# Attention steps in the order piece, score, score, piece, and the sum over experts as one strided reduction

## The chip, the cores and the metric

The kernel runs on one core of one Trainium2 chip. What is measured is the device time of one execution in microseconds. Three runs of the kernel before gave 3410.56, 3414.06 and 3416.23 us; the median is 3414.06.

## What is computed

A network of two layers over 3327 nodes with 256 features. Each layer adds a graph part (a product with the adjacency, in the second layer an attention over a graph) and a feed-forward part. The change lies in the feed-forward part of the second layer alone, which begins with a causal attention of four heads and four experts:

```python
def _L1_ffn_ref(x, hl_w, hl_b, wq, wk, wv, gate_w, gate_b, ln_g, ln_b, ...):
    b, s, h = x.shape                       # nh = 4 heads of d = 64, ne = 4 experts
    sx = jnp.einsum('bsh,ndh->bnsd', x, hl_w) + hl_b[None, :, None, :]
    q = jnp.einsum('bnsd,neod->bneso', sx, wq)
    k = jnp.einsum('bnsd,nod->bnso', sx, wk)
    v = jnp.einsum('bnsd,nod->bnso', sx, wv)
    scores = jnp.einsum('bnesd,bntd->bnest', q, k) * d ** 0.5 + causal
    att = jax.nn.softmax(scores, axis=-1)
    qkv = jnp.einsum('bnest,bntd->bnesd', att, v)
    out = jnp.transpose(qkv, (0, 1, 3, 2, 4)).reshape(b, nh, s, ne * d)
    gs = jax.nn.softmax(jnp.einsum('bnsf,nef->bnse', out, gate_w) + ..., axis=-1)
    mixed = jnp.einsum('bnsed,bnse->bnsd', out.reshape(b, nh, s, ne, d), gs)
    hn = layernorm(mixed + resid, ln_g, ln_b)
    ...
```

The last lines matter here: the outputs of the four experts are multiplied by their gate and summed into `mixed`.

## The kernel before

The whole network is one program of stages that follow each other with a barrier between. `stage_attention` (line 1587) takes about two thirds of the time. It handles two heads at a time, as two lanes of 64 partitions ("head pair" hp = 0, 1). The 3328 rows of queries are cut into seven blocks: block 0 has 256 rows, blocks 1 to 6 have 512. A **unit** is one block with one expert (block 0 puts two experts in a unit), so there are 26 units per head pair and 52 in all: unit 2 is block 1 with expert 0, unit 6 begins block 2, unit 10 block 3, 14 block 4, 18 block 5, 22 block 6; the second head pair repeats this from unit 26.

Inside a unit the keys are taken in groups of 128, from the first key to the diagonal. Two groups make a **step**: block b has 2b+1 steps (block 5 has 11). In the last two steps' worth of groups, on the diagonal, the columns shrink from 512 to 384, 256 and 128.

A step consists of these parts, which every engine handles in an order written out by hand:

- a **score** (`scores(g)`, lines 1748 to 1757): four pairs of matmuls that put the scores of one group, less the row's maximum, into a slot of `psR`. ScalarE turns it into exponentials in `at_pt` (`exps`, line 1840), of which there are four buffers. The scores of a step are those of the next step's groups.
- **values** (`values(g)`, line 1769): exponentials times V, into `psO`. Two groups a step, at its end.
- a **piece** (`row_max`, line 1730): the row's maximum must be known before its scores are made. So a step also computes, for the unit after next, cheap scores of one 128-row tile against 512 keys, into a slot of `psR`; VectorE takes the maximum over each lane (`at_mx`, line 1899). Most steps have two pieces, a few have three. `max_pieces(u, k, half)` gives the first piece for half 0 and the rest for half 1.
- **turns**: keys "k", queries "q", row of maxima "r", and output "t". They go through `psX`. The row of maxima and the two output turns fall in steps 1 and 2 of a unit, the query in its last step. For a query or key ScalarE makes the high half and VectorE the low half (lines 1888 and 1883).
- at the end of a unit VectorE takes the output out of `psO` (`take_out`, line 1920) and then the maxima over pieces (`maxima`, line 1909).
- GpSimd adds each group's exponentials to `at_acc` (lines 2026 and 2029), two additions a step; in the last two units VectorE does it.
- the **gate**, once per block, in the first unit of the next block: part 0 (step 2 of a long unit; VectorE, lines 1947 to 1960), part 1 (step 3; ScalarE, VectorE, and GpSimd's multiplication of the experts' outputs by their weights, line 2036), part 2 (step 4; VectorE sums the experts, adds the sum to `hn`, and takes statistics, lines 1971 to 1982). VectorE does a part behind the two maxima of its step. In blocks of three steps the parts fall elsewhere: block 0's parts 1 and 2 in step 0 of unit 3.

`psR` has three slots, which scores and pieces use in turn: `slot_users()` lists the users in order of issue, and `take_slot` makes the matmuls of each user wait until the user three places before it has been read (a score by its exp, a piece by its maximum):

```python
            i = slot_of[user]
            if i >= SLOTS:
                what, before = users[i - SLOTS]
                pe.wait_ge(p1_read if what == "max" else e_ready, before + 1)
```

## Time and profile before

| | before |
|---|---|
| median of three runs | 3414.06 us (3410.56 to 3416.23) |
| the profiled execution | 3411.35 us, its span 3409.6 us |
| mean granted TensorE clock in it | 0.938 |
| TensorE busy | 3022.5 us, 89% |
| VectorE busy | 1882.0 us, 55% |
| GpSimd busy | 1783.4 us, 52% |
| ScalarE busy | 1284.8 us, 38% |
| GpSimd's additions into `at_acc` | 674, mean 2159 ns |
| VectorE's maxima of pieces | 784, mean 1112 ns |
| exps | 776, mean 944 ns |

The table is a mean over all stages. Matmuls are pipelined, so a busy TensorE may still issue late; how far two matmuls start apart tells more than how long each is shown.

### The profile page before, as it was taken

To read this page: it belongs to the slowest core of one execution; us is meant where nothing else is said; L and a number is where in the kernel's file an instruction comes from. 1 tells how busy PE (TensorE), PEld (TensorE's weight loads), DVE (VectorE), ACT (ScalarE), POOL (GpSimd) and SP (SyncE) were. 2 spreads that over 40 slices of the span, in tenths; PEclk is the share of its full clock that TensorE was granted. 3 is DMA by queue.
4 is the path that set the end of the run, shared out by engine and by line. 5 is a ranking of instruction groups with operands and counts; after the bars stand their busy time and mean duration, and the time that the engine had idled before them with its cause. 6 is when DMAs were issued, how large, how long until landed. Compare 5 with 4: busy or idle time off the path is not lost. (4 is left out here: it accounts for less than half of the span.)

```text
span 3409.6 us, 46365 instructions
## 1 busy us (share of the span) xinstructions
PE 3022.5 (89%) x18170; PEld 1857.4 (54%) x18170; DVE 1882.0 (55%) x2869; ACT 1284.8 (38%) x1712; POOL 1783.4 (52%) x957
## 2 busy tenths in 40 slices
PE   7998987589998899999999999789899999999953
PEld 3467656378875555555545555455555554545532
DVE  3545764477833456564565641255656465565566
ACT  2232320355533234334434344233343443434433
POOL 0030020332311366777888889546777878888014
PEclk9999888899998899999999999889999999999976
DMA  9961100399960000000000000000000000000001
GB/s 390 423 233 48 55 1 8 112 295 268 267 118 3 1 1 1 1 1 1 1 1 1 1 1 1 1 1 1 1 1 1 1 1 1 1 1 1 1 3 40
DMA packets 63607, 195.24 MB, mean 57 GB/s; under 512 B 8228, under 2 KB 24994, under 8 KB 53411
## 3 DMA queue, kind: packets, MB, share of 16 engines
q1 hardware_dynamic: 38642, 147.98, 11.3%
q0 software_dynamic: 24752, 44.31, 7.2%
q8 instruction: 149, 2.44, 0.3%
q14 instruction: 64, 0.52, 0.0%
HBM read 188.86 MB, written 3.41 MB: 56 GB/s over the span
## 5 line engine op out<-in xcount | busy, mean ns | idle before, releaser
L2029 POOL TENSOR_TENSOR at_acc<-at_acc,at_pt 128x1024 f32<-128x1024 f32 (+3 forms) x674 | 1455.1, 2159 | 271.5 <-ACT at_pt L1840 197.1
L1899 DVE TENSOR_REDUCE at_mx<-at_psR 128x2 f32<-128x1024 f32 (+3 forms) x784 | 859.8, 1112 | 812.4 <-PE at_psR L1730 527.7
L1840 ACT ACTIVATE at_pt<-at_psR 128x1024 f32<-128x1024 f32 (+3 forms) x776 | 728.5, 944 | 971.9 <-PE at_psR L1751 624.3
L1769 PE MATMUL at_psO<-at_pt,v 128*64 128x512 f32 (+3 forms) x3104 | 697.8, 571 | 9.8 <-DVE at_oT L1920 9.8
L1748 PE MATMUL at_psR<-at_qhi,at_klo 64*128 64x512 f32 (+2 forms) x1552 | 344.3, 439 | 68.2 <-DVE at_mx L1899 61.9
L1730 PE MATMUL at_psR<-at_khi,at_qhi 64*128 64x512 f32 (+3 forms) x1568 | 341.8, 430 | 38.8 <-DVE at_mx L1899 9.0
L1769 PEld LDWEIGHTS at_psO<-at_pt,v 128*64 128x64 f32 x3104 | 190.7, 137 | 326.6 <-issue 271.1
L1316 PE MATMUL ga_acc<-h,ga_ring 128*128 128x257 f32 (+1 forms) x1352 | 305.1, 386 | 30.1 <-ACT ga_ring L1210 26.6
L1748 PEld LDWEIGHTS at_psR<-at_qhi,at_klo 64*128 64x128 f32 x1552 | 149.8, 188 | 323.5 <-issue 304.4
L1316 PEld LDWEIGHTS ga_acc<-h,ga_ring 128*128 128x128 f32 (+1 forms) x1352 | 257.9, 193 | 75.6 <-ACT ga_ring L1210 34.7
L1748 PE MATMUL at_psR<-at_qlo,at_khi 64*128 64x512 f32 (+2 forms) x1552 | 298.8, 380 | 0.0
L1751 PE MATMUL at_psR<-at_nm,at_ones_r 64*128 64x512 f32 (+2 forms) x1552 | 297.8, 378 | 0.0
L1748 PE MATMUL at_psR<-at_qhi,at_khi 64*128 64x512 f32 (+2 forms) x1552 | 297.8, 378 | 0.0
L1730 PEld LDWEIGHTS at_psR<-at_khi,at_qhi 64*128 64x128 f32 x1568 | 162.3, 189 | 169.9 <-issue 147.6
L1189 POOL DMA_DIRECT2D ga_ring<-in_adjT x91 | 110.2, 1381 | 250.9 <-DVE ga_ring L1252 245.7
L345 PE MATMUL gc_acc<-gc_cols,gc_xs 128*128 128x512 f32 x416 | 184.0, 605 | 21.7 <-DVE gc_xs L413 13.1
L1751 PEld LDWEIGHTS at_psR<-at_nm,at_ones_r 64*128 64x128 f32 x1552 | 151.0, 189 | 27.6
L1748 PEld LDWEIGHTS at_psR<-at_qhi,at_khi 64*128 64x128 f32 x1552 | 151.0, 190 | 27.1
L1210 ACT ACTIVATE ga_ring<-ga_ring,f 128x512 f32<-128x512 f32 (+1 forms) x182 | 114.7, 682 | 128.7 <-DMA ga_ring<-in_adjT 128.7
L1748 PEld LDWEIGHTS at_psR<-at_qlo,at_khi 64*128 64x128 f32 x1552 | 151.7, 191 | 12.9
L2026 POOL COPY at_acc<-at_pt 128x1024 f32<-128x1024 f32 x50 | 52.8, 1055 | 183.8 <-PE at_psX L1715 103.1
L345 PEld LDWEIGHTS gc_acc<-gc_cols,gc_xs 128*128 128x128 f32 x416 | 80.8, 195 | 124.1 <-issue 114.6
(331 smaller groups left out, 3442.3 us busy)
## 6 DMA issues: line engine op xcount, KB each, us to landing
gc_rows<-in_adj SPq DMA_DIRECT2D x26, 1664.0 KB, 17.4
ga_rows<-in_adj SPq DMA_DIRECT2D x26, 1664.0 KB, 10.0
ga_ring<-in_adjT POOLq DMA_DIRECT2D x78, 512.0 KB, 23.7
gc_cols<-in_adjT SPq DMA_DIRECT2D x26, 1024.0 KB, 14.9
gc_ring<-in_adjT SPq DMA_DIRECT2D x26, 512.0 KB, 8.0
gc_ring<-in_adjT SPq DMA_DIRECT2D x13, 256.0 KB, 2.8
ga_ring<-in_adjT POOLq DMA_DIRECT2D x13, 256.0 KB, 9.3
out_x<-X SPq DMA_DIRECT2D x6, 512.0 KB
```

The costliest lines, as they stand in the source:

```text
L345: ins = pe.matmul(acc[:, b, c, :], xs[:, t, c * P:(c + 1) * P], cols[:, t % COLS, b * BLK:(b + 1) * BLK], start=(t == 0), stop=(t == NT - 1))
L1189: pool.dma_start(ring[:, k, :, 0:w], srcT[:, k, :, c0:c0 + w], accum_op=ALU.add).then_inc(pair_added[k], 16)
L1210: ins = act.activation(ring[:, k, j, 0:w], ring[:, k, j, 0:w], ACT.Exp, bias=f20[:, 2 * k + j:2 * k + j + 1])
L1316: ins = pe.matmul(acc[:, bank(b, s), 0:DM + 1], ring[0:r, k, j, s * P:(s + 1) * P], h1[0:r, 2 * k + j, :], start=(k + j == 0), stop=last)
L1730: ins = pe.matmul(psR[:, slot, l, 0:w], qhi[lanes[l], u % 3, s * P:(s + 1) * P], khi[lanes[l], kc:kc + w], start=True, stop=not diag)
L1748: pe.matmul(packed(psR[:, slot, l, 0:w], g), left[lanes[l], kc:kc + P], columns(right[lanes[l], u % 3, :], g), start=first, stop=False)
L1751: ins = pe.matmul(packed(psR[:, slot, l, 0:w], g), ones_r[lanes[l], :], columns(nm[lanes[l], u % 2, :], g), start=False, stop=not diag)
L1769: ins = pe.matmul(columns(psO[lanes[l], :], g), v1[:, t, (2 * hp + l) * D:(2 * hp + l + 1) * D], packed(pt[:, g % PTS, l, 0:w], g), start= ...
L1840: act.activation(pt[:, g % PTS, :, 0:w], psR[:, slot_of["score", g] % SLOTS, :, 0:w], ACT.Exp).then_inc(e_ready, 1)
L1899: dve.tensor_reduce(mx[:, u % 2, :, s, c:c + 1].rearrange("p l o -> p (l o)"), psR[:, slot_of["max", i] % SLOTS, :, 0:w], AX.X, ALU.max).t ...
L2026: pool.tensor_copy(to, got).then_inc(added, 1)
L2029: pool.tensor_tensor(to, to, got, ALU.add).then_inc(added, 1)
```

## The change

The part of a step that issues scores and pieces goes from score, first piece, score, other pieces to first piece, score, score, other pieces. `slot_users()` follows, so the slots are handed out in the new order, and each user waits for another one. VectorE's and ScalarE's own orders of maxima and exps stay. In the gate's part 2, the two additions over experts become one `tensor_reduce` over a view whose innermost axis is the expert, written to a new tile `at_mixed`; the last block of the second head pair keeps two additions, of which the second writes `at_mixed`.

```diff
@@ slot_users
-            for half in range(2):
-                if g + 2 + half < FIRST[NU]:
-                    out.append(("score", g + 2 + half))
-                out += [("max", piece[0]) for piece in max_pieces(u, k, half)]
+            out += [("max", piece[0]) for piece in max_pieces(u, k, 0)]
+            out += [("score", x) for x in (g + 2, g + 3) if x < FIRST[NU]]
+            out += [("max", piece[0]) for piece in max_pieces(u, k, 1)]
@@ stage_attention, tiles
+        mixed = m.sb("at_mixed", [P, SUB, P])
@@ TensorE
-                        for half in range(2):
-                            if g + 2 < ng:
-                                scores(g + 2 + half)
-                            for piece in max_pieces(u, k, half):
-                                row_max(u + 2, *piece)
+                        for piece in max_pieces(u, k, 0):
+                            row_max(u + 2, *piece)
+                        if g + 2 < ng:
+                            scores(g + 2)
+                            scores(g + 3)
+                        for piece in max_pieces(u, k, 1):
+                            row_max(u + 2, *piece)
@@ VectorE, gate part 2
-                        link(dve.tensor_tensor(on[:, 0:ws, 0:2, :], on[:, 0:ws, 0:2, :], on[:, 0:ws, 2:4, :], ALU.add))
-                        link(dve.tensor_tensor(on[:, 0:ws, 0, :], on[:, 0:ws, 0, :], on[:, 0:ws, 1, :], ALU.add))
+                        if at_block < NPR * NQB - 1:
+                            link(dve.tensor_reduce(mixed[:, 0:ws, :], on[:, 0:ws, :, :].rearrange("p s e c -> p s c e"),
+                                                   AX.X, ALU.add))
+                        else:
+                            link(dve.tensor_tensor(on[:, 0:ws, 0:2, :], on[:, 0:ws, 0:2, :], on[:, 0:ws, 2:4, :], ALU.add))
+                            link(dve.tensor_tensor(mixed[:, 0:ws, :], on[:, 0:ws, 0, :], on[:, 0:ws, 1, :], ALU.add))
-                        dve.tensor_tensor(hsl, hsl, on[:, 0:ws, 0, :], ALU.add).then_inc(mix_done, 1)
+                        dve.tensor_tensor(hsl, hsl, mixed[:, 0:ws, :], ALU.add).then_inc(mix_done, 1)
```

TensorE, step 3 of unit 20 (block 5), before. L1748 and L1751 are a score, L1730 is a piece, L1769 is values:

```order
L1748 MATMUL at_psR<-at_qhi,at_klo 128x512 x2
L1748 MATMUL at_psR<-at_qlo,at_khi 128x512 x2
L1748 MATMUL at_psR<-at_qhi,at_khi 128x512 x2
L1751 MATMUL at_psR<-at_nm,at_ones_r 128x512 x2
L1730 MATMUL at_psR<-at_khi,at_qhi 128x512 x2
L1748 MATMUL at_psR<-at_qhi,at_klo 128x512 x2
L1748 MATMUL at_psR<-at_qlo,at_khi 128x512 x2
L1748 MATMUL at_psR<-at_qhi,at_khi 128x512 x2
L1751 MATMUL at_psR<-at_nm,at_ones_r 128x512 x2
L1730 MATMUL at_psR<-at_khi,at_qhi 128x512 x2
L1769 MATMUL at_psO<-at_pt,v 64x512 x4
```

The same step in the change:

```order
L1730 MATMUL at_psR<-at_khi,at_qhi 128x512 x2
L1748 MATMUL at_psR<-at_qhi,at_klo 128x512 x2
L1748 MATMUL at_psR<-at_qlo,at_khi 128x512 x2
L1748 MATMUL at_psR<-at_qhi,at_khi 128x512 x2
L1751 MATMUL at_psR<-at_nm,at_ones_r 128x512 x2
L1748 MATMUL at_psR<-at_qhi,at_klo 128x512 x2
L1748 MATMUL at_psR<-at_qlo,at_khi 128x512 x2
L1748 MATMUL at_psR<-at_qhi,at_khi 128x512 x2
L1751 MATMUL at_psR<-at_nm,at_ones_r 128x512 x2
L1730 MATMUL at_psR<-at_khi,at_qhi 128x512 x2
L1769 MATMUL at_psO<-at_pt,v 64x512 x4
```

The first piece moved ahead of the first score; the second piece and values stand where they were.

VectorE, steps 4 and following of unit 18, with the gate's part 2, before. L1899 are the maxima of pieces, `at_on` the experts' outputs:

```order
L1967 TENSOR_TENSOR at_wgt<-at_gs,at_rden 128x32
L1899 TENSOR_REDUCE at_mx<-at_psR 128x2 x2
L1971 TENSOR_TENSOR at_on<-at_on 128x4x256
L1972 TENSOR_TENSOR at_on<-at_on 128x4x128
L1974 TENSOR_TENSOR hn<-hn,at_on 128x4x128
L1978 BN_STATS at_hn_stats<-hn 128x6 x8
L1982 BN_AGGR hn_mv<-at_hn_stats 128x2 x8
L1899 TENSOR_REDUCE at_mx<-at_psR 128x2 x12
```

The same place in the change, whose line numbers there are two to six higher:

```order
L1969 TENSOR_TENSOR at_wgt<-at_gs,at_rden 128x32
L1901 TENSOR_REDUCE at_mx<-at_psR 128x2 x2
L1974 TENSOR_REDUCE at_mixed<-at_on 128x512
L1980 TENSOR_TENSOR hn<-hn,at_mixed 128x4x128
L1984 BN_STATS at_hn_stats<-hn 128x6 x8
L1988 BN_AGGR hn_mv<-at_hn_stats 128x2 x8
L1901 TENSOR_REDUCE at_mx<-at_psR 128x2 x12
```

Two additions became one reduction, and the gate stands between the same maxima as before.

## Rows read from the trace of the kernel before

**Rows 1.** The page, part 1: busy us (share of span) x instructions.

```profile
PE 3022.5 (89%) x18170; PEld 1857.4 (54%) x18170; DVE 1882.0 (55%) x2869; ACT 1284.8 (38%) x1712; POOL 1783.4 (52%) x957
```

**Rows 2.** Busy by stretch: PE, PEld, DVE, ACT, POOL, clock, DMA share, GB/s.

```profile
1725.00:1730.00 5.00, 4.12 (x22) 3.30 (x24) 3.18 (x4) 1.35 (x2) 4.73 (x2) 0.60 0.00 0
...
1752.00:1808.00 56.00, 54.77 (x374) 29.76 (x374) 27.49 (x30) 24.04 (x30) 47.85 (x23) 1.00 0.00 1
2057.00:2115.00 58.00, 55.45 (x390) 29.93 (x386) 2.77 (x5) 26.93 (x33) 53.57 (x24) 1.00 0.00 1
```

**Rows 3.** Timeline, PE, unit 19: start us, length us, engine, line, out<-in, count.

```profile
1780.41 0.50 PE L1730 MATMUL at_psR<-at_khi,at_qhi 64*128 64x512 f32 x2
1780.84 1.94 PE L1769 MATMUL at_psO<-at_pt,v 128*64 128x512 f32 x8
...
1784.65 0.39 PE L1751 MATMUL at_psR<-at_nm,at_ones_r 64*128 64x512 f32 x2
1785.11 0.50 PE L1730 MATMUL at_psR<-at_khi,at_qhi 64*128 64x512 f32 x2
1785.55 0.65 PE L1769 MATMUL at_psO<-at_pt,v 128*64 128x512 f32 x2
```

**Rows 4.** Timeline, ScalarE and VectorE, same place; in brackets idle before, and releaser.

```profile
1779.24 2.16 ACT L1840 ACTIVATE at_pt<-at_psR 128x1024 f32<-128x1024 f32 x2 [2.65 <-PE at_psR L1751]
...
1785.65 1.23 DVE L1899 TENSOR_REDUCE at_mx<-at_psR 128x2 f32<-128x1024 f32 x1 [0.25 <-PE at_psR L1730]
```

**Rows 5.** Timeline, PE, unit 24: values of two steps without pieces.

```profile
2076.80 1.94 PE L1769 MATMUL at_psO<-at_pt,v 128*64 128x512 f32 x8
...
2080.71 0.65 PE L1769 MATMUL at_psO<-at_pt,v 128*64 128x512 f32 x2
```

**Rows 6.** Timeline, VectorE and PE, unit 18, around the gate.

```profile
1706.77 0.19 DVE L1960 TENSOR_TENSOR at_gl<-at_gl,at_gm 128x32 f32<-128x32 f32 x1
...
1713.74 3.39 DVE L1971 TENSOR_TENSOR at_on<-at_on 128x1024 f32<-128x1024 f32 x1
...
1719.94 2.71 DVE L1974 TENSOR_TENSOR hn<-hn,at_on 128x512 f32<-128x512 f32 x1
...
1724.51 2.36 DVE L1899 TENSOR_REDUCE at_mx<-at_psR 128x2 f32<-128x1024 f32 x2
...
1725.88 0.80 PE L1748 MATMUL at_psR<-at_qhi,at_klo 64*128 64x512 f32 x2 [6.18 <-DVE at_mx L1899]
...
1729.81 1.94 PE L1769 MATMUL at_psO<-at_pt,v 128*64 128x512 f32 x8
```

**Rows 7.** Timeline, VectorE and PE, from unit 18 to unit 19.

```profile
1751.08 1.23 DVE L1899 TENSOR_REDUCE at_mx<-at_psR 128x2 f32<-128x1024 f32 x1
...
1752.02 0.50 PE L1730 MATMUL at_psR<-at_khi,at_qhi 64*128 64x512 f32 x2
```

**Rows 8.** VectorE: a group (mean ns), one line (min/median/max ns), timeline of unit 26.

```profile
L2012 DVE TENSOR_TENSOR at_on<-at_on,at_wgt 128x2048 f32<-128x2048 f32 x1 | 2.3, 2291 | 0.0
...
L1954 DVE TENSOR_REDUCE at_gl<-at_gp x14: 261/391/399, 1150.9 to 3261.0; 128x32 f32<-128x128 f32 x12, 128x16 f32<-128x64 f32 x2
...
2202.91 2.02 DVE L1971 TENSOR_TENSOR at_on<-at_on 128x1024 f32<-128x1024 f32 x1 [3.73 <-POOL at_on L2036]
...
2206.64 0.69 DVE L1974 TENSOR_TENSOR hn<-hn,at_on 128x512 f32<-128x512 f32 x1
```

**Rows 9.** Timeline: unit 6's gate; TensorE behind it; TensorE behind unit 3's gate.

```profile
1243.46 1.24 DVE L1971 TENSOR_TENSOR at_on<-at_on 128x1024 f32<-128x1024 f32 x1
...
1249.98 3.68 PE L1769 MATMUL at_psO<-at_pt,v 128*64 128x512 f32 x8 [4.08 <-DVE at_oT L1920]
...
1165.98 0.80 PE L1748 MATMUL at_psR<-at_qhi,at_klo 64*128 64x512 f32 x2 [5.75 <-DVE at_mx L1899]
```

**Rows 10.** GpSimd's additions: a group (busy, mean ns, idle before); timeline of three.

```profile
L2029 POOL TENSOR_TENSOR at_acc<-at_acc,at_pt 128x1024 f32<-128x1024 f32 x532 | 1270.8, 2389 | 237.4 <-ACT at_pt L1840 181.4 <-POOL at_acc L2029 1.7
...
2065.27 7.42 POOL L2029 TENSOR_TENSOR at_acc<-at_acc,at_pt 128x1024 f32<-128x1024 f32 x3
```

## The prediction

> **What bounds the kernel now.** I read the page's busy line first [rows 1]: TensorE is busy 89% of the span, GpSimd 52%, VectorE 55%. Those are averages over stages, so the next view was the busy time by stretch [rows 2]. In attention (1,080 to 3,260 us) TensorE has next to no idle time inside a long unit at its full granted clock: 54.77 of 56 us in unit 19, with GpSimd at 47.85. In unit 24, which has almost no pieces to run, GpSimd is at 53.57 of 58. So TensorE bounds most units and GpSimd stands close behind. Busy is not the same as useful here, so I looked at one step of unit 19 instruction by instruction [rows 3]. Its values start at 1780.84 and the next values at 1785.55: 4.71 us a step. Pairs of 512 columns follow each other every 0.23 us, but between the last pair of the second score (1784.65) and the second piece (1785.11) lie 0.46 us, and the piece then takes 0.43 instead of 0.32 to hand over to values. That piece takes the PSUM slot of the step's first score, three uses earlier, and waits for its exp. The ScalarE row of the step before shows the same place [rows 4]: two exps from 1779.24, the first done near 1780.33, the piece at 1780.41. In unit 24 a step without pieces takes 3.91 [rows 5]. Two pieces at 0.23 each would make it 4.37. **So a plain step loses 0.34 us to that wait.** The other thing to see is where VectorE is late [rows 6]: after a gate it is blocked for 10.8 us, and TensorE stands still before the score at 1725.88.
>
> **The order of a step.** Now it is score 0, piece 0, score 1, piece 1; after, piece 0, score 0, score 1, piece 1, then turns and values as before. With three slots each user waits for the one three before it. Call T the start of the first matmul after values. Piece 0 now waits for the first exp of the step before, score 0 for the second exp, score 1 for the second maximum of the step before; all of these are done by then (second exp near T+3.7, next step at T+4.37). Piece 1 waits for piece 0's maximum of the same step. From the rows: the maximum starts 0.55 after a piece that follows values or another wait (1785.11 to 1785.65) and takes 1.23 [rows 3, 4], so with 0.07 for the hand-over it is done at T+1.85. Piece 1 is wanted at T+0.34+8x0.23 = T+2.2. **The margin is 0.35 us, and any VectorE work that delays piece 0's maximum by more stops TensorE.** Before, that maximum was wanted only by the next step's score 0, some 3.4 us after its own piece had ended.
>
> 1. Plain steps, where VectorE is idle when piece 0 ends: -0.33 each. Units of block b have 2b+1 steps; steps 3 to 2b-2 are plain. Outside the gated units that is 2, 4 and 6 steps in blocks 3, 4, 5, three units each, both head pairs: 72; then 4 in the gated units of block 5, 12 in units 48 and 49. 88 x 0.33 = -29.
> 2. Steps 1 and 2 (with the turns) have the same wait, partly hidden by short pieces: -0.53 for both together, by the same gaps. 26 units of blocks 3 to 6 and 6 ungated of block 2: -17.
> 3. The last two steps and the first of the next unit. In the step with scores of 256 and 128 columns the scores are too short to cover the maximum: +0.2. At the unit's end VectorE does the query's low half, the output and the maxima [rows 7]: it comes free at 1751.08, and piece 0's maximum, which now is the next thing TensorE needs, ends near 1752.05 even with all else 0.3 earlier. Piece 1 goes at 1752.1 where it went at 1752.02, so the 0.33 gained in the last step is given back: +0.1. Together +0.3 in 34 units: +10.
> 4. The gate's sum. The two additions that go take 6.2 us beside GpSimd's additions (1713.74 to 1719.94) and 3.7 free of them (2202.91 to 2206.64) [rows 6, 8]; the addition into `hn` stays, at 2.71 and 0.69. The new reduction reads 2048 elements, four per result at a stride of 128. No row shows it. From below: one pass over 2048 elements along the row, the multiplication of line 2012, takes 2.3. From above: the nearest strided reduction is `at_gp` into `at_gl`, also over experts, with 391 ns for 128 elements and 261 for 64, a slope of 2.0 each [rows 8]; 2048 elements then take 4.1 to 4.3. I take **4.1**, since it has the same pattern, and keep a quarter more (5.3) as the far end. The gate step is then 2.0 shorter where GpSimd is busy, and 0.4 longer where the additions ran free.
> 5. What the gate costs in the new order, in unit 18. Its first part ends at 1706.96 [rows 6]: piece 0's maximum of step 3 follows at 1708.1, so values of step 3 start 1.1 later than before. The last part then starts at 1714.65 instead of 1713.74, takes 8.75 instead of 10.75 and ends at 1723.4, before at 1724.5. Before, values of step 5 ran inside the stall; now piece 1 of step 5 waits for the first maximum, so it goes at 1724.8, and values (1.87), a whole new step (2.5 to its values) and the low clock after the stall (mean granted clock 0.60 from 1725 to 1730 [rows 2], part of it at the 1.2 GHz level; about 1.5 us lost there, in both orders) follow: next values at 1731.0, before at 1729.81 [rows 6]. +1.2 a gate, seven gates in blocks 3, 4, 5 and unit 48: +8.4.
> 6. Block 2's gates (units 6 and 32) have nearly free additions (1.24 the first), with the output behind them, which values of the next unit wait for [rows 9]. The gate ends up to 1.5 later, and values of unit 7, at 1249.98 now, come behind output, maxima and piece 0's maximum, so 1.9 after their old place; with 1 us from the first part and the gains of steps 1 and 2 off, +3.8 each, +7.6.
> 7. The first block's gates (units 3 and 29): the reduction of 1024 saves 2.6, but piece 1, turn and values now lie behind the stall before 1165.98 instead of inside it [rows 9]: +0.8 each. Unit 26: +0.5. Together +2.
> 8. Block 6 of the first head pair (units 22 to 25) is GpSimd's: 2.39 us an addition and 0.14 between [rows 10], two a step against 4.37. TensorE's gain goes into the wait for a free `at_pt`: -1 in all.
> 9. The last block keeps its two additions; the table of slots, ScalarE's and GpSimd's order are as before. The 2 KB tile costs nothing.
>
> **The sum:** -29 -17 +10 +8.4 +7.6 +2 -1 = -19. The profiled execution took 3411.4, so 3392; the median of the runs is 2.7 higher: **3395**.
>
> **What the Trainium skill says.** The rows show 2.0 ns an element for a strided reduction against 1.1 for a pass along the row [rows 8]. "Vector Engine (DVE) Microarchitecture Reference", section 5.2, says a port streams at the full rate only over runs of two or more adjacent words, and gives 1.73 ns a column for one source hopping at every element, about 2.5 for small steps. By it the reduction would take 3.6 to 5.2, and the sum would be -24 to -7. "SBUF — State Buffer", section Who interferes with whom, says that a reduction never contends with GpSimd where an addition of two SBUF inputs does; by that rule the removed additions' excess is really saved. The trace agrees on the additions: 3.39 beside GpSimd and 2.02 in unit 26 for the same shape [rows 6, 8].
>
> **The rivals.**
> - *The reduction streams.* It takes 2.3: 1.8 less in ten gates, 0.9 in two. The sum is then -39, 3375. For it: only four reads per output, and the small rows carry a large fixed part. Against: the slope between 64 and 128 elements.
> - *The exchange comes out even.* The plain steps gain, but the unit ends and gates (items 3, 5, 6, 7: 28) cost half as much again, because VectorE's queue also holds the key's and query's low halves, or GpSimd's backlog (5.0 a step against 4.4) takes some of the gain of blocks 4 and 5: +14 on the sum, 3409. For it: [rows 10] and the buffer of four. Against: over a whole unit of block 5 GpSimd needs 50.8 (18 x 2.53, a copy, the narrow ones) and TensorE still 53.5 (55.7 less items 1 to 3).
> - *Slower: piece 1 waits for VectorE in every step.* If piece 0's maximum ends 0.35 later than I set it, the wait just changes its releaser; items 1 and 2 fall to nothing while items 3, 5, 6 and 7 stay: +46 on the sum, 3441. It decides at T+2.2. Against: the maximum's start and length are regular to 0.02 in the rows. For: the margin is thin and appears some 120 times.
> - *The change does little:* the waits found above are modelled ends of matmuls, not time. Against: the step without pieces really takes 3.91.
>
> **How the numbers follow.** Forecast 0.45; streaming reduction 0.2; even 0.2; slower 0.15. The predicted time is the forecast's. Faster by over 0.2% (below 3407) takes the first two and a quarter of the third: 0.7; within 0.2% (3407 to 3421, about what a measurement of this kernel can tell from no change) 0.15; slower 0.15. The range runs from the streaming case with some margin, 3370, to 3418, which takes in the dear reduction (5.3: +13) and the even case, and leaves out the slower rival.
>
> **What would show it.** In the profile after: plain steps of unit 19 at 4.37 to 4.4 between values, with 0.23 before piece 1; if they stay at 4.7 and piece 1 has VectorE's maximum as releaser, the slower rival holds. The new reduction's mean at 4.1 settles item 4. Values of unit 18 some 12 to 14 us apart around the gate, with TensorE standing before a piece instead of a score, show item 5; the first values of a unit 0.4 later behind the last of the unit before shows item 3. In unit 23 ScalarE should wait more for GpSimd. Wrong would be, above all, an unseen cost in block 1, whose steps I did not work out one by one.

## The result

| | before | after |
|---|---|---|
| median of the runs | 3412.31 us (3404.88 to 3416.23, 4 runs) | 3378.77 us (3376.77 to 3385.28, 4 runs) |
| after / before | | 0.9908, 95% interval 0.9885 to 0.993 |
| span of the profiled execution | 3409.6 us | 3375.0 us |
| mean granted TensorE clock | 0.938 | 0.937 |

The change makes the kernel 33.5 us faster. That is inside the range and between the forecast (3395) and the rival of the streaming reduction (3375). The runs below show that the total came out near for other reasons than the sum's: the reduction alone is worth 38 us, and the new order costs 3.4 us by itself and 5.7 on top of the reduction.

The page of after, part 1 (busy us, share of the span, instructions), and three groups of part 5 (out<-in, count, busy us, mean ns, idle before them and its main releaser):

```profile
PE 2975.5 (88%) x18170; PEld 1844.0 (55%) x18170; DVE 1851.5 (55%) x2856; ACT 1253.4 (37%) x1712; POOL 1772.8 (53%) x957
...
L2035 POOL TENSOR_TENSOR at_acc<-at_acc,at_pt 128x1024 f32<-128x1024 f32 (+3 forms) x674 | 1445.8, 2145 | 273.4 <-ACT at_pt L1842 195.3
L1901 DVE TENSOR_REDUCE at_mx<-at_psR 128x2 f32<-128x1024 f32 (+3 forms) x784 | 864.4, 1113 | 805.3 <-PE at_psR L1730 520.8
...
L1730 PE MATMUL at_psR<-at_khi,at_qhi 64*128 64x512 f32 (+3 forms) x1568 | 354.5, 446 | 126.7 <-DVE at_mx L1901 93.7
```

TensorE's busy time fell by 47 against [rows 1], VectorE's by 30.5. The last line shows the price of the order: TensorE stands 93.7 us before pieces for VectorE's maxima. What TensorE waits for, by line, in after (us in total, times, longest), where before the same list began with 61.9 us before scores in 10 waits:

```profile
PE at_psR L1730 <- DVE at_mx L1901: 93.7, 62, 7.0
...
PE at_psR L1730 <- DVE at_qlo L1890: 26.7, 41, 1.4
```

The plain step, on TensorE and then on VectorE (start us, length us, engine, line, out<-in, count, in brackets the idle time before and its releaser):

```profile
1762.29 1.94 PE L1769 MATMUL at_psO<-at_pt,v 128*64 128x512 f32 x8
1764.15 0.50 PE L1730 MATMUL at_psR<-at_khi,at_qhi 64*128 64x512 f32 x2
...
1766.13 0.39 PE L1751 MATMUL at_psR<-at_nm,at_ones_r 64*128 64x512 f32 x2
1766.36 0.40 PE L1730 MATMUL at_psR<-at_khi,at_qhi 64*128 64x512 f32 x2
```

```profile
1764.70 1.23 DVE L1901 TENSOR_REDUCE at_mx<-at_psR 128x2 f32<-128x1024 f32 x1 [1.08 <-PE at_psR L1730]
```

Against [rows 3], the second piece now follows the score after 0.23 us. The first maximum ends at 1765.93, T+1.78, and the piece that needs its slot goes at T+2.21: no wait, as worked out. Most plain steps take 4.38 us where they took 4.71; those that took 4.66 or 4.84 take 4.32 and 4.52.

The gate of unit 18, on VectorE and on TensorE behind it (answers to [rows 6]):

```profile
1705.84 3.83 DVE L1974 TENSOR_REDUCE at_mixed<-at_on 128x512 f32<-128x2048 f32 x1
1709.71 1.50 DVE L1980 TENSOR_TENSOR hn<-hn,at_mixed 128x512 f32<-128x512 f32 x1
1711.25 1.11 DVE L1984 BATCH_NORM_STATS2 at_hn_stats<-hn 128x6 f32<-128x64 f32 x8
1712.39 0.64 DVE L1988 BATCH_NORM_AGGREGATE hn_mv<-at_hn_stats 128x2 f32<-128x6 f32 x8
1713.07 1.23 DVE L1901 TENSOR_REDUCE at_mx<-at_psR 128x2 f32<-128x1024 f32 x1
```

```profile
1714.44 0.80 PE L1730 MATMUL at_psR<-at_khi,at_qhi 64*128 64x512 f32 x2 [5.75 <-DVE at_mx L1901]
1715.17 3.68 PE L1769 MATMUL at_psO<-at_pt,v 128*64 128x512 f32 x8
1718.78 0.79 PE L1730 MATMUL at_psR<-at_khi,at_qhi 64*128 64x512 f32 x2
```

Part 2 takes 7.2 us instead of 10.8: the reduction 3.83 for 3.39 and 2.73, the addition onto `hn` 1.50 for 2.71. TensorE stands before a piece, as forecast, and values come behind the stall, at the lower clock: 3.68 us for eight matmuls that take 1.94 in the plain step.

### The profile page after: what moved, and what is told of

Its sections match the earlier page's. It is cut to its first block and busy times, and to the rows that moved or that the text cites. A ratio compares the mean times of both kernels' runs of the same rounds, so it can differ in the third digit from the quotient of the medians.

```text
span 3375.0 us, 46352 instructions
## 1 busy us (share of the span) xinstructions
PE 2975.5 (88%) x18170; PEld 1844.0 (55%) x18170; DVE 1851.5 (55%) x2856; ACT 1253.4 (37%) x1712; POOL 1772.8 (53%) x957
## 5 line engine op out<-in xcount | busy, mean ns | idle before, releaser
L1842 ACT ACTIVATE at_pt<-at_psR 128x1024 f32<-128x1024 f32 (+3 forms) x776 | 697.4, 942 | 1006.3 <-PE at_psR L1751 693.5
L1769 PE MATMUL at_psO<-at_pt,v 128*64 128x512 f32 (+3 forms) x3104 | 714.2, 582 | 0.3 <-ACT at_pt L1842 0.3
L1730 PE MATMUL at_psR<-at_khi,at_qhi 64*128 64x512 f32 (+3 forms) x1568 | 354.5, 446 | 126.7 <-DVE at_mx L1901 93.7
L1769 PEld LDWEIGHTS at_psO<-at_pt,v 128*64 128x64 f32 x3104 | 193.5, 140 | 331.1 <-issue 238.2
L1730 PEld LDWEIGHTS at_psR<-at_khi,at_qhi 64*128 64x128 f32 x1568 | 155.2, 187 | 400.6 <-issue 345.2
L1748 PE MATMUL at_psR<-at_qhi,at_klo 64*128 64x512 f32 (+2 forms) x1552 | 312.7, 399 | 4.2 <-ACT at_pt L1842 3.9
L1748 PE MATMUL at_psR<-at_qlo,at_khi 64*128 64x512 f32 (+2 forms) x1552 | 294.8, 375 | 0.0
L1748 PE MATMUL at_psR<-at_qhi,at_khi 64*128 64x512 f32 (+2 forms) x1552 | 293.7, 374 | 0.0
L1751 PE MATMUL at_psR<-at_nm,at_ones_r 64*128 64x512 f32 (+2 forms) x1552 | 292.3, 372 | 0.0
L1748 PEld LDWEIGHTS at_psR<-at_qhi,at_klo 64*128 64x128 f32 x1552 | 149.5, 189 | 50.8 <-issue 37.0
L1748 PEld LDWEIGHTS at_psR<-at_qhi,at_khi 64*128 64x128 f32 x1552 | 148.5, 187 | 27.4
L1751 PEld LDWEIGHTS at_psR<-at_nm,at_ones_r 64*128 64x128 f32 x1552 | 148.1, 186 | 27.4
L1748 PEld LDWEIGHTS at_psR<-at_qlo,at_khi 64*128 64x128 f32 x1552 | 149.3, 188 | 24.2
```

The source lines that it names most:

```text
L1730: ins = pe.matmul(psR[:, slot, l, 0:w], qhi[lanes[l], u % 3, s * P:(s + 1) * P], khi[lanes[l], kc:kc + w], start=True, stop=not diag)
L1748: pe.matmul(packed(psR[:, slot, l, 0:w], g), left[lanes[l], kc:kc + P], columns(right[lanes[l], u % 3, :], g), start=first, stop=False)
L1751: ins = pe.matmul(packed(psR[:, slot, l, 0:w], g), ones_r[lanes[l], :], columns(nm[lanes[l], u % 2, :], g), start=False, stop=not diag)
L1769: ins = pe.matmul(columns(psO[lanes[l], :], g), v1[:, t, (2 * hp + l) * D:(2 * hp + l + 1) * D], packed(pt[:, g % PTS, l, 0:w], g), start= ...
L1842: act.activation(pt[:, g % PTS, :, 0:w], psR[:, slot_of["score", g] % SLOTS, :, 0:w], ACT.Exp).then_inc(e_ready, 1)
```

## The experiments

Blocks, units and steps are compared from their first values to the first values of the next. All times are us; the kernel before ran on the same chip each time (medians 3411.5 to 3413.6). None of the kernels leaves work out; three add an instruction.

**The two parts alone.** `e1_order` keeps the new order and puts the additions back; `e2_reduce` keeps the reduction and puts the old order back.

```diff
@@ e1_order, gate part 2
-  link(dve.tensor_reduce(mixed[:, 0:ws, :], on[:, 0:ws, :, :].rearrange("p s e c -> p s c e"), AX.X, ALU.add))
+  link(dve.tensor_tensor(on[:, 0:ws, 0:2, :], on[:, 0:ws, 0:2, :], on[:, 0:ws, 2:4, :], ALU.add))
+  link(dve.tensor_tensor(on[:, 0:ws, 0, :], on[:, 0:ws, 0, :], on[:, 0:ws, 1, :], ALU.add))
@@ e2_reduce, TensorE (slot_users alike)
-  pieces of half 0; scores(g + 2); scores(g + 3); pieces of half 1
+  scores(g + 2); pieces of half 0; scores(g + 3); pieces of half 1
```

> The new order of piece, score, score, piece alone; the sum over experts stays with its two additions. Theory A (the parts add, and the gate's part 2 lies on the path in either order): the trace of the changed kernel shows part 2 in unit 18 3.5 us shorter (7.2 against 10.8), seven such gates, 2.6 each in units 3 and 29 and about 1 longer in units 6 and 32. The order alone then gives about 27 less than the whole gain of 33: -6, some 3406, ratio 0.998, with plain steps at 4.38. Theory B (the prediction's sizes: part 2 only 2.0 shorter, order the larger part): order alone -17, some 3395, ratio 0.995.

> The strided reduction alone, in the old order of score, piece, score, piece. Theory A: part 2 is 3.5 shorter here too and the stall behind it shrinks by as much: -24 to -28, some 3386, ratio 0.992 to 0.993, plain steps still at 4.71. Theory B: the addition into hn still waits 2.7 beside GpSimd, part 2 is 2.3 shorter: -12 to -16, some 3398, ratio 0.996.

Measured: order alone 3414.85 against 3411.46, ratio 1.0014 (1.0005 to 1.0023); reduction alone 3373.06, ratio 0.9884 (0.987 to 0.9897). Both theories missed both: the order alone doesn't gain, and the reduction alone gains more than the two together. The two effects nearly add up: +3.4 and -38.4 make -35, and both together measured -33.5.

One thing bears on every small difference below. Attention's first matmul comes between 1070.8 and 1078.1 us after the start in these traces (1072.3 before, 1070.9 in the change, 1076.9 with the reduction alone), and nothing that the kernels do differently stands ahead of it. So differences of a few us between two medians say little. From that matmul to the last values attention takes 2182.3 before, 2183.2 with the order alone, 2139.4 with the reduction alone and 2148.7 with both.

The order alone at unit 18's gate shows where its gain goes, on TensorE:

```profile
1717.87 1.94 PE L1769 MATMUL at_psO<-at_pt,v 128*64 128x512 f32 x8
1731.35 0.80 PE L1730 MATMUL at_psR<-at_khi,at_qhi 64*128 64x512 f32 x2 [9.29 <-DVE at_mx L1901]
1732.08 3.68 PE L1769 MATMUL at_psO<-at_pt,v 128*64 128x512 f32 x8
```

It stands 9.29 us, before it was 6.18 [rows 6]; the long part of the gate is uncovered 3 us earlier, since the piece needs the first maximum of its own step. Unit 18 takes 65.6 instead of 62.6; units 19 to 21, which have no gate, are 2.2, 1.6 and 1.6 shorter. With the reduction and the old order the stall is 2.62, shorter by just the 3.5 that the gate's part 2 lost, and the step's values are through before it:

```profile
1707.11 1.94 PE L1770 MATMUL at_psO<-at_pt,v 128*64 128x512 f32 x8
1711.67 0.50 PE L1749 MATMUL at_psR<-at_qhi,at_klo 64*128 64x512 f32 x2 [2.62 <-DVE at_mx L1900]
```

The granted clock stays at 1.00 through this stretch, the 2.4 GHz level (its rows stand in the last section), where before it fell to a mean of 0.60 behind 6.18 us [rows 2]. That fits a stall shorter by 3.5 making unit 18 shorter by 4.6 (62.6 to 58.0), so that the reduction is worth more than the time it saves on VectorE. Over all eight gates of this kind, from the values of step 2 to those of step 6 in the first units of blocks 3 to 6, TensorE takes 221.9 us before, 186.0 with the reduction alone, 251.5 with the order alone and 224.0 with both. So the reduction makes nearly all of its gain at these gates (-35.9), and the order loses there (+29.7) what it gains elsewhere.

**The units' ends.** `e3_step0_old` is the changed kernel with the old order in the first step of each unit alone (TensorE and `slot_users` ask one function for the order).

```diff
+def piece_first(u, k):
+    return k > 0
```

> The changed kernel, but the first step of every unit has the old order. In the changed kernel its values come 4.02 after the values before, 3.64 in the kernel before. Theory A (in that step piece 0 waits for the query's low half, and piece 1 for VectorE's output, maxima and piece 0's maximum; a score ahead hides both): the step goes back to 3.65 to 3.7, 0.33 less in some 44 units, -12 to -15 against the changed kernel, ratio to the kernel before 0.987. Rival: the time is VectorE's queue at the unit's end whatever the order, and the step stays at 4.0: no change against the changed kernel.

Measured 3363.29, ratio 0.9862 (0.9848 to 0.9875), 15.5 below the changed kernel. The interval from a unit's last values to the next unit's first is 3.64 again; it is 4.00 to 4.03 in the changed kernel. So the price that item 3 put on the first step, 0.33 and 0.1, is about right (0.38). Its mechanism was another; this is the first step of unit 20 in after:

```profile
1793.84 0.87 PE L1769 MATMUL at_psO<-at_pt,v 128*64 128x256 f32 x8
1795.32 0.50 PE L1730 MATMUL at_psR<-at_khi,at_qhi 64*128 64x512 f32 x2 [0.61 <-DVE at_qlo L1890]
```

The first piece, not the second, waits: it needs the low half of the next query, which VectorE begins only at 1794.57, while a score doesn't.

**Blocks 1 and 2.** `e4_blocks12_old` is the changed kernel with the old order in those blocks.

```diff
+def piece_first(u, k):
+    return b not in (1, 2)
```

> The changed kernel, but the units of blocks 1 and 2 have the old order. Between the first values of block 1 and of block 3 the changed kernel takes 4.8 + 1.8 us longer than the one before in the first head pair, 4.4 + 1.4 in the second. Theory A (that is the order, whose losses the short blocks' few plain steps do not pay back): those units fall below the kernel before, since the shorter part 2 stays, 8 to 16 us below the changed kernel in all, ratio to the kernel before 0.987. Rival: it is the reduction, slower where the additions ran free (units 6, 32) and in units 3 and 29: then the units stay as long as in the changed kernel.

Measured 3375.89, ratio 0.9896 (0.9883 to 0.991): 2.9 below the changed kernel, within the spread, so theory A's 8 to 16 is not there. Block 2 takes 119.4 twice (changed 119.2 and 118.8, before 117.4 twice, the reduction alone 118.1 and 119.3, the order alone 116.9 and 118.3): there the rival is right, the order comes out about even and the loss comes with the reduction, which in units 6 and 32 replaces two short additions (1.24 us [rows 9] and 1.11) by 3.80. Block 1 takes 86.9 and 85.6 (changed 89.2 and 88.9, before 84.4 twice, the reduction alone 80.8 and 84.6), so the old order inside it wins back 2.3 and 3.3.

The rest is TensorE's clock and not a wait. These are busy times and granted clock (columns as in [rows 2]) of the same two intervals, from the values of the second step of block 1's second unit to the first values of the next unit: in the first head pair of the kernel `e11_split_mixed_b0old` below (old order in blocks 0 and 1), then in `e6_split_mixed` (new order in block 0 alone of the two), and last in the second head pair of `e5_split_old` (old order everywhere):

```profile
1160.56:1178.40 17.84, 13.64 (x91) 8.62 (x91) 9.61 (x23) 6.00 (x10) 9.28 (x7) 0.90 0.00 1
```

```profile
1155.00:1175.62 20.62, 16.43 (x91) 10.05 (x90) 9.85 (x23) 6.01 (x10) 9.46 (x7) 0.75 0.00 1
```

```profile
2221.90:2241.28 19.38, 15.14 (x91) 8.78 (x91) 9.84 (x23) 6.01 (x10) 9.45 (x7) 0.82 0.00 1
```

TensorE stands idle for 4.2 us in each; what grows is the time of the same matmuls, at a lower mean clock. In the first head pair the two intervals are long in the two kernels with the new order in block 0 and the old one in block 1 (20.6 and 20.7) and short in the three with the reduction and the old order in both (17.8). In the second head pair `e5_split_old`, with the old order in both, is at 19.4 like the first two. So in these rows block 0 hands no wait on to block 1; whether its order brings on the lower clock stays open.

**The gate cut in two.** What is left of the stall should be the length of one uninterrupted stretch of VectorE. `e5_split_old` is the reduction with the old order, and the addition onto `hn` with its statistics stands one step later, as a part 3.

```diff
@@ which gate parts stand in step k
-  return [(hp, b, i) for i in range(3) if k == 2 + i]
+  return [(hp, b, i) for i in range(4) if k == 2 + i]
@@ gate, piece 2: wait, reduction; piece 3:
+  else:
       hsl = hn[:, c0 // P:c0 // P + ws, hp * P:(hp + 1) * P]
       dve.tensor_tensor(hsl, hsl, mixed[:, 0:ws, :], ALU.add)
```

> Reduction kept, order of before (score, piece, score, piece), and the gate's last part cut in two: the reduction over the experts stands one step ahead of the addition onto hn with its statistics. Against the run with the reduction alone (3373). Theory A (what is left of the gate's stall is the length of one uninterrupted VectorE stretch, 7.2 us, against some 5 us of cover): two stretches of about 3.9 and 3.3 us fit under the cover, the step of 7.40 us in unit 18 falls to 5.0 to 5.6 and the sum of the four steps around it from 22.4 to at most 20.8; with seven full gates and the smaller ones 12 to 22 us off, 3351 to 3361. Rival B (the stall is VectorE's whole work around the gate, not how it is cut): the sum of the four steps stays at 22 to 22.5 and the time within 4 us of 3373. Rival C (the addition lands one step later, beside a GpSimd instruction, and waits longer for it): part three takes over 4.5 us and the time stays above 3365.

`e10_after_split` does the same to the changed kernel.

> The changed kernel (piece, score, score, piece everywhere) with the gate's last part cut in two as before. Theory A (TensorE's stall of 5.75 us behind the gate in unit 18 is the 7.2 us stretch less a cover of some 1.5): the two stretches of 3.9 and 3.6 us stall it 2.0 to 2.8 and 1.0 to 2.5, the two steps that took 10.68 + 6.88 take 12.5 to 14.5, and eight gates of this kind make the whole 24 to 38 lower than the changed kernel, 3341 to 3355. Rival B (two stalls add up to the one): the two steps 16.5 or more, the whole within 8 of 3379. Either way it stays above the kernel with mixed order (3300), since block 1, the units' first steps and the gates keep the order that costs there.

Measured: 3358.19 (3349.33 to 3360.69), ratio 0.9843 (0.9827 to 0.986), and 3348.28 (3343.73 to 3352.94), ratio 0.9814 (0.9799 to 0.9829). By the totals theory A in both: 14.9 off the reduction alone, 30.5 off the changed kernel. With the old order the waits for maxima are gone around the gate; what TensorE waits for there is an exp (unit 18):

```profile
1691.18 0.50 PE L1733 MATMUL at_psR<-at_khi,at_qhi 64*128 64x512 f32 x2 [0.82 <-ACT at_pt L1843]
1691.61 1.94 PE L1772 MATMUL at_psO<-at_pt,v 128*64 128x512 f32 x8
1696.21 0.50 PE L1733 MATMUL at_psR<-at_khi,at_qhi 64*128 64x512 f32 x2 [0.41 <-ACT at_pt L1843]
```

The step of 7.40 takes 5.03. But the four intervals behind it take 5.25, 5.08, 4.61 and 6.52 where they took 4.66, 4.83, 3.95 and 5.63, and unit 18 as a whole takes 58.1 where it took 58.0. Behind the gate GpSimd now works without a gap, its multiplication first and then 14 additions, and the exps wait for buffers that its additions free:

```profile
1683.92 3.62 POOL L2045 TENSOR_TENSOR at_on<-at_on,at_wgt 128x2048 f32<-128x2048 f32 x1 [4.38 <-DVE at_wgt L1970]
1687.50 32.07 POOL L2038 TENSOR_TENSOR at_acc<-at_acc,at_pt 128x1024 f32<-128x1024 f32 x14
```

So in the old order the cut takes the stall away and GpSimd becomes the limit of the gated unit. Blocks 5 and 6 change by next to nothing (+0.1 and -0.9, 0.0 twice); what the cut gives in the old order lies in blocks 2 (-3.2 and -5.9), 3 (-3.4 and -2.2) and 4 (-1.8 and -2.0). In the new order the stall of 5.75 becomes one of 2.37, and the two steps that took 10.68 and 6.88 take 7.03 and 6.02:

```profile
1700.28 0.50 PE L1732 MATMUL at_psR<-at_khi,at_qhi 64*128 64x512 f32 x2 [2.37 <-DVE at_mx L1903]
1700.71 3.32 PE L1771 MATMUL at_psO<-at_pt,v 128*64 128x512 f32 x8
```

With the gate cut, the new order is the faster one by the medians, 3348 against 3358; the single runs overlap, and attention takes 2117.3 in its trace against 2121.3. With the gate in one piece it was the slower one, 2148.7 against 2139.4. So its verdict hangs on what else stands in VectorE's queue.

**The order where it pays.** `e6_split_mixed` is the cut gate with the new order in block 0 and in the steps of blocks 2 to 6 where the traces show a gain, the old one elsewhere.

```diff
+def piece_first(u, k):
+    return b == 0 or (b > 1 and k > 0 and k != ls - 2
+                      and not (e == 0 and k in (3, 5, 6))
+                      and not (b == 2 and e == 1 and k < 2))
```

> As the split kernel, but in the order piece, score, score, piece at the steps where the traces show it to pay (block 0 and the plain steps of blocks 2 to 6), and the order of before in block 1, in a unit's first step and its last but one, around the gate (steps 3, 5 and 6 of a block's first unit) and at the start of block 2's second unit. Theory A (each step's price by order is local and adds up): plain steps at 4.38 instead of 4.71, some 70 of them, minus 18 to minus 25 against the split kernel in the old order, so 3330 to 3342 if that gives 3355. Rival B (a change of order inside a unit costs a shift of its own, or the cover saved up by long steps is what the old-order steps live on): less than 10 us off it, above 3345.

Measured 3299.84 (3294.91 to 3301.72), ratio 0.9667 (0.9653 to 0.9682): 58 below the old order with the cut gate, 79 below the changed kernel. It lies far outside the expectation of 3330 to 3342, which counted only the plain steps. In the trace nearly every step that is switched gains: of unit 19's eleven intervals nine fall by 0.2 to 0.4, for 2.9 in all (55.8 to 52.9). By kind of interval the two traces differ in attention by -24 in the plain steps outside the gated units, -19 in steps 1 and 2, -14 in the units' last steps, -4 in the plain steps of gated units, +6 in the narrow and first steps (the gated units' alone) and +1 in blocks 0 and 1: -53, of which the span shows 50. So the expectation had the plain steps right and left out steps 1 and 2 and the last ones. TensorE's wait list begins with nothing of VectorE's maxima any more. In attention it now reads:

```profile
PE at_psR L1748 <- ACT at_pt L1858: 21.0, 27, 1.7
...
PE at_psR L1748 <- DVE at_qlo L1906: 8.1, 8, 1.4
PE at_psR L1766 <- ACT at_pt L1858: 7.8, 14, 1.1
PE at_psR L1748 <- DVE at_mx L1917: 7.4, 14, 0.6
```

`e11_split_mixed_b0old` takes block 0's one step back to the old order.

```diff
-    return b == 0 or (b > 1 and k > 0 ...)
+    return b > 1 and k > 0 ...
```

> The mixed kernel with block 0's one step in the order of before too. In the traces block 0 is 1.6 (and 3.3 in the second half) faster in the new order, but block 1 behind it 5.9 slower with it (13.60 + 4.25 against 14.54 + 6.09 in unit 3). Theory A (the new order in block 0 only moves the wait for the gate's row into block 1): first half 4 to 7 us better, second half within 2, the whole 3 to 8 below the mixed kernel, 3292 to 3297. Rival B (what block 0 loses is lost): blocks 0 and 1 together as before, the whole 3298 to 3306.

Measured 3303.73 (3298.51 to 3307.8), ratio 0.9687 (0.9671 to 0.9704): rival B's figure, but the runs overlap the mixed kernel's (3294.91 to 3301.72). In its trace attention's first matmul comes 5.5 later than in the mixed kernel's, ahead of any step whose order differs. From there to block 2 it takes 139.9 where the mixed kernel takes 145.8, and blocks 0 and 1 of the second head pair are 2.0 shorter, as theory A had it for the two halves. Its mechanism fails all the same: no wait moved, the idle times in the two intervals of block 1 shown above are equal and the granted clock differs. Which of the two orders is better in block 0 stays open.

**The margin of piece 1.** `e7_delay32` and `e8_delay512` are the changed kernel with one more VectorE instruction ahead of the maximum of each step's first piece; `e9_before_delay512` is the kernel before with the longer of them.

```diff
@@ VectorE, row_max
     dve.wait_ge(p1_full, i + 1)
+    if i in firsts:
+        dve.tensor_reduce(idle_out[:, :], <32 or 512 values of hn>, AX.X, ALU.max)
```

> The changed kernel with one more VectorE instruction, a maximum over 32 values (about 0.19 us), after the wait and ahead of the maximum of every step's first piece. Theory A (in a plain step the second piece is reached 0.35 us after the first piece's maximum has released its slot): 0.19 us fits, plain steps stay at 4.38 (up to 4.42), and TensorE still stands before the first piece of the step; the whole grows by 0 to 15 us, at gates and units' ends only. Rival B (there is no margin, the 0.35 is an artefact of modelled ends): plain steps 4.52 to 4.57, the span 3400 or more.

> The same with a maximum over 512 values (about 0.69 us). Theory A (margin 0.35 us, then one for one): plain steps 4.38 + 0.34 = 4.72 (4.65 to 4.80), TensorE now standing before the step's second piece for VectorE's maximum at L1905 or so, some 88 plain steps times 0.34 = +30 and as much again at the other steps: the span 3425 to 3450. Rival B (the slots' release isn't what binds, ScalarE's exponential is): plain steps stay under 4.50 and the span under 3400.

> The kernel before with the same added maximum over 512 values (0.69 us) ahead of every step's first piece. Theory A (in the old order the second score stands between the two pieces, so a late maximum has about 2 us more cover): plain steps stay at 4.71 (up to 4.76), where the same instruction took the changed kernel's from 4.38 to 4.81; the whole grows at the gates and in steps that VectorE bounds, 3412 to 3450, less than half of the 118 us that it cost the changed kernel. Rival B (VectorE binds the old order's steps as well): plain steps 4.9 or more, the whole above 3470.

Measured 3378.72, 3498.41 and 3479.06, one run each (the added instruction 0.186 and 0.686 at the median). With 0.19 plain steps stay at 4.38, and the whole doesn't move. With 0.69 they take 4.80:

```profile
1817.55 0.69 DVE L1905 TENSOR_REDUCE at_idle_out<-hn 128x1 f32<-128x512 f32 x1 [1.07 <-PE at_psR L1731]
1818.16 1.22 DVE L1906 TENSOR_REDUCE at_mx<-at_psR 128x2 f32<-128x1024 f32 x1
```

```profile
1817.01 0.50 PE L1731 MATMUL at_psR<-at_khi,at_qhi 64*128 64x512 f32 x2
...
1818.96 0.39 PE L1752 MATMUL at_psR<-at_nm,at_ones_r 64*128 64x512 f32 x2
1819.52 0.50 PE L1731 MATMUL at_psR<-at_khi,at_qhi 64*128 64x512 f32 x2 [0.17 <-DVE at_mx L1906]
1819.95 1.94 PE L1770 MATMUL at_psO<-at_pt,v 128*64 128x512 f32 x8
```

The maximum starts 0.60 later than in the changed kernel (T+1.15 for T+0.55) and ends at T+2.37, 0.19 behind the piece's turn at T+2.18. The step is 0.43 longer: 0.33 before the piece and 0.10 in the hand-over to values. So a wait that only just binds costs 0.43 here for an excess of 0.19. The margin is real and of the size worked out: 0.60 less 0.19 to the maximum's end, 0.34 with the hand-over of 0.07. The whole grew by 122 (spans), not by the 50 to 75 of theory A: the steps that already wait have no margin, 4.21 to 4.80 in the step with narrow scores and 4.02 to 4.61 in a unit's first, in nearly every unit of blocks 3 to 5. In the old order plain steps stay at 4.71 with the same instruction, but the whole grew by 68, more than theory A gave it; rival B had the time right and the mechanism wrong. Steps that run three pieces went from 5.27 to 5.87, the last step of the third and fourth expert's units from 6.00 to 6.59, and block 1 from 84.4 to 95. The old order covers the first maximum only where the step has two pieces.

## Why the prediction was right in its total and wrong in its shares

By stretches (after less before in the two traces, and what the items came to):

| | measured | items |
|---|---|---|
| up to the end of block 1, both head pairs | -0.6 | about +2 |
| block 2, both | +3.2 | +7 |
| block 3, both | -5.8 | -3 |
| block 4, both | -10.8 | -7 |
| block 5, both | -11.1 | -13 |
| block 6, first head pair | -5.0 | -1 |
| block 6, second | -4.7 | -3 |

Of the first row, -1.4 lies ahead of attention's first matmul.

The prediction added the two parts gate by gate and never priced them apart. The expectations of the first two runs did so afterwards, in their theory B: -17 for the order and -12 to -16 for the reduction, which is already more than its -19. Measured were +3.4 and -38.4, one 20 worse and the other 22 or more better. So it is luck that the total lies within 16 of the forecast.

- **Item 1**, plain steps: price exact (4.71 to 4.38), count too high. Of the steps counted as plain, one or two in each unit of the third and fourth expert run a third piece (5.28 to 5.12 and 5.32 to 5.06 in unit 16, 5.26 to 5.12 and 5.09 to 5.08 in unit 20) and gain 0.01 to 0.26. The 88 intervals together come to -27.0 for -29.
- **Item 2**: right in block 5, where unit 19 goes from 6.74 to 6.40 and from 7.40 to 7.20, -0.54 for -0.53. In unit 16 it is 6.74 to 6.41 and 6.39 to 6.52, -0.2. Its 64 intervals together come to -17.3 for -17.
- **Item 3**: size about right, mechanism partly another (the query's low half), shown by the run with step 0 in the old order (-15.5). For +0.3 a unit the ungated units of blocks 3 to 5 show +0.2 to +0.5 (unit 19 +0.30, unit 20 +0.45), those of block 2 -0.2.
- **Item 4** is the term that was mis-sized. The reduction takes 3.80 for 4.1, and the addition behind it 1.50 for 2.71, which I had kept. Part 2 is 3.5 shorter, not 2.0. The traces show why the kept term moved. These are the GpSimd additions that run when unit 18's addition onto `hn` starts, before (it starts at 1719.94) and after (at 1709.71):

```profile
1719.50 2.60 POOL L2029 TENSOR_TENSOR at_acc<-at_acc,at_pt 128x1024 f32<-128x1024 f32 x1
```

```profile
1708.31 2.35 POOL L2035 TENSOR_TENSOR at_acc<-at_acc,at_pt 128x1024 f32<-128x1024 f32 x1
```

VectorE's addition ends 0.55 behind the end of that GpSimd addition in both (1722.65 behind 1722.10, 1711.21 behind 1710.66). Before, three additions stood in a row: each ended just behind one of GpSimd's (the first, of 1024 values, 1.08 behind one that ended at 1716.05, the second 0.55 behind 1719.35), so the next began with most of a GpSimd addition still ahead of it. The reduction isn't held up so, and the one addition left begins in the middle of one. It also answers the prediction's figure for additions "free" of GpSimd: in unit 26 a copy and a narrow addition of GpSimd run beside them, and the second one, of 512 values, took 1.63 where 0.69 is the time alone. The groups of after (count, busy us, mean ns, idle before):

```profile
L1974 DVE TENSOR_REDUCE at_mixed<-at_on 128x512 f32<-128x2048 f32 x11 | 41.8, 3799 | 6.0 <-POOL at_on L2042 5.4
L1980 DVE TENSOR_TENSOR hn<-hn,at_mixed 128x512 f32<-128x512 f32 x12 | 16.6, 1385 | 0.4
L1974 DVE TENSOR_REDUCE at_mixed<-at_on 128x256 f32<-128x1024 f32 x2 | 3.8, 1920 | 4.0 <-POOL at_on L2042 4.0
```

- **Item 5**: direction and place right, size too high. The values of step 2 and step 6 of unit 18 stand 27.81 apart where they stood 27.04 apart; +0.8 for +1.2. In the seven gates counted it is -0.2 to +0.8, together +1.6 for +8.4, the largest miss of the sum, and it comes from item 4. In unit 18 two errors work against each other: part 2 is 1.5 shorter than I worked out, and the lower clock now runs over values (3.68 for 1.94) as well as over the score behind them. The order's real price at a gate is that of the two reduction kernels: 27.8 against 22.4, 5.4 us in unit 18 (3.8 to 5.7 in the eight gates), hidden from me since I compared with the long gate only.
- **Items 6 and 7**: blocks 0 to 2 as a whole came out better than forecast by 6, of which 1.4 lies ahead of attention; block by block they were wrong. Block 0 gained 7.7, which I had at nothing. Part of it is TensorE's clock: the first unit takes 22.2 us at a mean granted clock of 0.58 before, 19.8 to 20.0 at 0.70 to 0.71 in the four other kernels with the old order there and the reduction, 17.3 to 17.5 at 0.79 to 0.80 in the change and three more kernels with the new order. In the new order TensorE has a piece to run after the row of maxima, while ScalarE copies the row, where before it stood 0.68 and then ran that step's scores at the lower level, pairs 0.43 apart for 0.23. How much of the gain the order makes is not shown. Block 1 lost 9.3, of which the old order inside the block wins back 5.6. Block 2 lost 3.2: its gated unit 6 takes 3.2 more where item 6 said 3.8, and its other units win 1.4 back.
- **Item 8**: GpSimd's additions of block 6 run 258.8 us from the first to the last where they ran 260.9, so GpSimd's own part is -2.1. The other 3 lie in the last interval to unit 26 (23.3 to 20.3). That interval is 18.5 to 23.3 in the kernels here and follows neither part of the change. Its mean granted clock is 0.67 before and 0.78 after, which goes with the 3 us; what sets it stays open.
- **The rivals.** The slower one was excluded by its own mark, T+2.2, and the delay run shows that it would have held with 0.69 more on VectorE. The even one named the right weights (unit ends and gates dearer than the forecast), and the order alone, at +3.4, is nearly that case. Streaming was not it: 1.86 ns an element against 1.1.

On the pages cited ahead: the 3.80 us of a reduction that hops at every element lies inside the 3.6 to 5.2 that came from "Vector Engine (DVE) Microarchitecture Reference", section 5.2, of the Trainium skill, near its single-source figure (1.73 ns a column; measured 1.86). Its figure of about 2.5, the upper end, is for both sources or the output in small steps, and no run here has that case. And the trace agrees with its "SBUF — State Buffer", section Who interferes with whom: the reduction takes 3.83 in unit 18, where GpSimd is busy for 3.69 of it, and 3.67 in unit 26, where it is busy for 2.21 (before, the addition of 1024 took 3.39 and 2.02 [rows 6, 8]).

## What to carry to other kernels

A reorder that removes a small wait in every step should be priced against the longest uninterrupted stretch of the engine that the new order leans on. Look for what else stands in its queue, shorten or cut that first (the cut alone was worth 30 us in the new order, 15 in the old, where GpSimd then set the pace of the gated units), and take the new order only where the queue is empty: the mixed kernel with the cut gate is 3.3% faster than before, the uniform one 0.9% (1.9% with the cut gate). And when two edits are made together, run each alone, since here the one that looked like the smaller term carried the whole gain. Where two kernels differ by a few us, compare stretches of their traces, and the granted clock in them, before naming a cause.

## What the hardware showed that I had not expected

- A VectorE addition of two SBUF inputs that starts while one of GpSimd's additions runs ends a fixed time behind the end of that one, whenever it started. The additions onto `hn` show 0.54 to 0.55 us for 512 values and 0.28 for 256, in all the gates of before and after in which GpSimd is busy (in units 6 and 32 of before it is a copy of GpSimd's). The time behind grows with the addition's size, as if it had done nothing while GpSimd's ran. The 128x512 addition onto `hn` so took 0.69 free, 1.50 in after's unit 18, 2.71 before, and 0.82 to 2.82 in the changed kernel with the cut gate. Even 32 values show it: this row of the changed kernel ends 0.05 behind a GpSimd addition that ended at 1697.77, where 0.19 is its time undisturbed.

```profile
1695.96 1.86 DVE L1958 TENSOR_TENSOR at_gl<-at_gl,at_gb 128x32 f32<-128x32 f32 x1
```

- Stalls of the same length left the clock at different levels. The granted clock by stretch (columns as in [rows 2]) behind the stall of 2.37 in the changed kernel with the cut gate, and then behind the one of 2.62 in the old order with the reduction:

```profile
1698.00:1700.20 2.20, 0.00 (x0) 0.00 (x0) 2.10 (x2) 0.72 (x2) 2.06 (x2) 1.00 0.00 0
1700.20:1702.00 1.80, 1.72 (x6) 0.65 (x8) 1.18 (x2) 0.80 (x1) 1.80 (x1) 0.76 0.00 0
1702.00:1704.00 2.00, 2.00 (x8) 0.28 (x4) 1.97 (x10) 0.00 (x0) 1.86 (x2) 0.50 0.00 0
```

```profile
1709.00:1711.60 2.60, 0.05 (x2) 0.00 (x0) 2.53 (x15) 0.04 (x1) 2.46 (x2) 1.00 0.00 0
1711.60:1714.00 2.40, 2.33 (x18) 1.80 (x18) 1.92 (x2) 1.03 (x1) 2.26 (x2) 1.00 0.00 0
```

The first fell to 0.50, the 1.2 GHz level, and its eight values matmuls took 3.32 for 1.94; the second stayed at 1.00. No run tells the two apart, so a short stall may cost 1.4 us more than its length or nothing more. Behind stalls below 1 us every values group around this gate took 1.94 or less. In block 1 the same steps with the same idle times took 17.8 to 20.6 us at a mean granted clock of 0.90 to 0.75 (the rows under blocks 1 and 2).
